# A graph network's sort and degree count: a search moved from one stage to the next

## The chip, the core and the metric
The kernel runs on one core of a Trainium2 chip. The metric is the device time of one execution in microseconds (us). The engines are named as in the profile: PE is TensorE, DVE is VectorE, ACT is ScalarE, POOL is GpSimd, SP is SyncE.

## The reference
`x` holds 12500 nodes of 16 numbers, `src` and `dst` 400000 edges between them, sorted by `dst`. The first layer runs a small MLP on each edge's two ends, makes a Householder reflection of each result, and adds messages to both ends; the second is a graph convolution applied twice. Both scale by degrees:
```
deg   = zeros(n).at[src].add(1).at[dst].add(1)          # layer 1: both ends
coef  = 1/sqrt(max(deg, 1e-5))[src] * 1/sqrt(...)[dst]
deg   = segment_sum(1, col) + 1 (self loop)             # layer 2: dst alone
norm  = rsqrt(deg)[row] * rsqrt(deg)[col]
```
Each layer is added to its input and normalized over the 16 numbers.

## The kernel before
The kernel handles gathers and scatters through a sorted order of the edges. Nodes are counted as 98 columns of 128 (`NB` = 98), two columns make a block of 256 nodes (`NW` = 49 blocks), and each of the 128 partitions holds 3125 edges (`EP`). The stages ahead of the graph layers are these.

- **Count.** The number of edges that leave each node is counted with one-hot matrices: DVE makes them for 25 edges of each partition at a time (`one_hots`, lines 1246 to 1254), ACT makes a part of them as sign steps (L694), and PE multiplies them (`count_group`, L987 and L990). There are 125 such groups (`GROUPS`) in two buffers; a DVE group waits on `hot_free` for the group two before it.
- **Search.** As `dst` is sorted, the number of edges that enter a node follows from the position of its first edge. POOL and DVE find it for all 98 x 128 nodes. PE first counts in which partition each falls (`ps_firsts`). Then there are four searches (`PROBES`), for the two halves of the 98 columns (`HALF` = 49) in 56 samples of the partition, and again for both in the 56 edges after the sample. For each, POOL issues 49 indirect DMAs (gathers, L601) into `found`, each with one index for each of the 128 partitions, and DVE compares and sums (`probe`, L1265 to L1276). DVE's loop over the groups is cut into five parts (`PAIRS`), with a search behind each of the first four, so that the gathers run beside the loop.
- **Borders.** From the first edges of every second column `cut_rows` (L1285 to L1316) finds how the edges of each block fall into rows of 5248 (`WID`); POOL gathers the keys of the edges into `keys` (41 gathers).
- **Degrees.** After the last group DVE adds the counts and makes both inverse roots, with ACT's square root in between (`rsqrt`, L1344 to L1354).
- **Sort.** Each row's 5248 keys are sorted by a merging network of 91 steps. In a step DVE takes the minimum and the maximum of two halves (L1386, L1387, two float32 inputs each) and ACT copies what doesn't move (L718, L719). The last 13 steps have no copies by ACT. `sort_stepped` counts the steps.
- **Lists.** POOL writes 99 indirect DMAs (L619) that mark where runs begin, and DVE waits for the lists (L1556).
- **Row expansion** (1420 to 2380 us): for each of 128 rows SP loads and stores about 2 MB, PE multiplies, ACT copies and DVE chooses (`choose`, L1617). SP's store of a row waits on `row_chosen`.

The graph layers follow, to the end. All order between engines is written out by hand with semaphores; each engine runs its instructions in order.

Of the kernel before, what the change touches and what calls it, by code (L numbers as in the profile page):

```python
# [11 lines left out]
def gnn_kernel(nc, x, src, dst, mlp_w1, mlp_b1, mlp_w2, mlp_b2, gcn_w1, gcn_b1, gcn_w2, gcn_b2, out):  # L12
# [9 lines left out]
    P = 128  # L22
    N, D = x.shape
# [52 lines left out]
    with ctx:  # L76
# [43 lines left out]
        dis = sb("dis", [P, NB])  # L120
        dinv = sb("dinv", [P, NB])
# [17 lines left out]
        place = sb("place", [P, WID], of=po)  # L139
        pa = ExitStack()  # L140
# [5 lines left out]
        follow = sb("follow", [P, P], of=pa)  # L146
        wrap = sb("wrap", [P, P], of=pa)
# [8 lines left out]
        found = sb("found", [P, HALF, BLOCK], of=pa)  # L156
        zeros = sb("zeros", [P, 2 * NB], of=pa)
        node_id = sb("node_id", [P, NB], of=pa)
        cum = sb("cum", [P, NB], of=pa)
        cnt = sb("cnt", [P, 2, NB], of=pa)  # L160
        start = sb("start", [P, NB + 1], of=pa)
        probe_i = sb("probe_i", [P, NB], I32, of=pa)
# [73 lines left out]
        iota_w = sb("iota_w", [P, LW], of=pb)  # L236
        pb.close()
# [82 lines left out]
        ps_edge = ps[:, 4 * BANK:4 * BANK + NB + 1]  # L320
# [35 lines left out]
        probe_ready, found_got = sem("probe_ready"), sem("found_got")  # L356
        start_ready, next_ready, edge_ready = sem("start_ready"), sem("next_ready"), sem("edge_ready")
# [21 lines left out]
        row_copied_seen, row_chosen = sem("row_copied_seen"), sem("row_chosen")  # L379
# [65 lines left out]
        sorted_keys = keys[sum(n + 1 for n in range((WID - 1).bit_length())) % 2]  # L445
        spare_keys = keys[1 - sum(n + 1 for n in range((WID - 1).bit_length())) % 2]
# [5 lines left out]
        def _(sp):  # L452
# [116 lines left out]
        def _(pool):  # L569
# [97 lines left out]
        def _(act):  # L667
# [38 lines left out]
            root(1)  # L706
            root(2)

# [15 lines left out]

            act.wait_ge(cuts_ready, 1)
# [203 lines left out]
            root(3)  # L929
# [41 lines left out]
            root(4)  # L971

        @block.tensor
        def _(pe):
# [4 lines left out]
            mm(ps_firsts, ones[:, :], hi_before[:, :], start=False, stop=True).then_inc(firsts_counted, 1)  # L979
# [12 lines left out]

            with pe.Fori(0, PAIRS[PROBES]) as i:
                for e in range(2):
                    count_group(i * 2 + e, e)
            pe.wait_ge(consts_ready, 1)
            pe.wait_ge(start_ready, 1)
            mm(ps_edge, first[:, :], start[:, :], start=True, stop=True).then_inc(edge_ready, 1)
            mm(ps_next, follow[:, :], start[:, 0:NB], start=True, stop=False)
            mm(ps_next, wrap[:, :], start[:, 1:NB + 1], start=False, stop=True).then_inc(next_ready, 1)  # L1000
            with pe.Fori(PAIRS[PROBES], GROUPS // 2) as i:
                for e in range(2):
                    count_group(i * 2 + e, e)
# [8 lines left out]
            mm(ps_rowat, ones[:, :], row_diag[:, :], start=True, stop=True).then_inc(rowat_ready, 1)  # L1012
            pe.wait_ge(runs_ready, 1)
# [191 lines left out]
        def _(dve):  # L1205
# [30 lines left out]
            v.tensor_scalar(hi_before[:, :], iota_f[:, 0:NB], first_lohi[:, 1:2], None, ALU.is_gt).then_inc(firsts_ready, 1)  # L1236
# [21 lines left out]
            dve.wait_ge(firsts_counted, 1)  # L1258
            step(v.tensor_scalar(part[:, :], ps_firsts, -1.0, 0.0, ALU.add, ALU.max))
            v.tensor_copy(probe_i[:, :], part[:, :]).then_inc(probe_ready, 1)  # L1260

            def probe(s):
                cols = slice(s % 2 * HALF, (s % 2 + 1) * HALF)
                dve.wait_ge(found_got, 16 * HALF * (s + 1))
# [17 lines left out]
            def cut_rows():  # L1282
                dve.wait_ge(keys_stored, 16)
                dve.wait_ge(edge_ready, 1)
                step(v.tensor_copy(edge[:, :], ps_edge[:, 0:NB + 1:2]))  # L1285
# [35 lines left out]
            for s in range(PROBES + 1):  # L1321
                with dve.Fori(PAIRS[s], PAIRS[s + 1]) as i:
                    for e in range(2):
                        dve.wait_ge(hot_free, i * 2 + (e - 1))
                        one_hots(e, i * (2 * T) + e * T)
# [591 lines left out]
```

## Time and profile before
| | |
|---|---|
| time, median of 3 runs | 7817.33 us (7814.12 to 7823.55) |
| span of the profiled execution | 8142.6 us |
| DVE busy | 7026.3 us, 86% |
| ACT, PE, POOL busy | 65%, 65%, 41% |
| count stage (41 to 676 us) | 635 us, DVE busy in 384.3 |
| sort (700 to 1160 us) | 460 us, DVE busy in 456.5 |

The profiled execution is one of its own, taken by the hardware profiler. Its span is 325 us longer than the median of the runs without it. Rows of the timeline give the start in us from the span's start, the duration, engine, line, operation and operands, and in brackets how long the engine had been idle and what released it. "issue" stands for idle time in which the engine waited for nothing that the profile shows, "remote" for a release whose sender the profile doesn't place on any engine.

### The profile page before, as it was taken

Reading aid. Unit: us, or ns where it says so; the run is one execution under the profiler, and the core shown is the slowest. Engines: PE = TensorE matmul, PEld = TensorE weight load, DVE = VectorE, ACT = ScalarE, POOL = GpSimd, SP = SyncE. Lnnn points to the kernel's source line nnn. Section 1 sums busy time; section 2 is a strip of 40 time slices with the busy share of each in tenths; the row PEclk is TensorE's granted clock in tenths of the full one; section 3 lists DMA queues with packets and bytes.
Section 4 is the critical chain, followed back from the end, with each engine's and each line's share of the span. In section 5 each row is a group of like instructions: output and inputs, shape, how many; then the busy total and the mean of one; then the engine's idle time right before and its main releaser. Section 6 shows DMA issues by size and latency. Waiting matters only on the chain.

```text
span 8142.6 us, 284433 instructions
## 1 busy us (share of the span) xinstructions
PE 5258.0 (65%) x105060; PEld 4635.4 (57%) x105060; DVE 7026.3 (86%) x9716; ACT 5313.1 (65%) x12774; POOL 3318.7 (41%) x2217
## 2 busy tenths in 40 slices
PE   3431000677759899999999987566466666566665
PEld 2321000566647777777777776555455566555665
DVE  6559993555559999999999999999899999999999
ACT  4534130222228888888888887888666788567886
POOL 3340006666643333333333332555200788101886
PEclk8655555888878777778777777555566555566555
DMA  3000000888863333333333332333499433697333
GB/s 45 12 20 5 0 13 13 307 292 299 294 225 99 105 105 103 104 103 104 104 105 105 105 104 84 94 85 85 112 295 296 123 94 94 199 295 237 94 94 78
DMA packets 510651, 1043.86 MB, mean 128 GB/s; under 512 B 125636, under 2 KB 316420, under 8 KB 497508
## 3 DMA queue, kind: packets, MB, share of 16 engines
q1 hardware_dynamic: 376804, 761.05, 27.3%
q0 software_dynamic: 113856, 281.66, 13.7%
q10 hardware_dynamic: 19904, 0.13, 0.2%
q8 instruction: 38, 0.62, 0.0%
q14 instruction: 49, 0.40, 0.0%
HBM read 756.40 MB, written 286.18 MB: 128 GB/s over the span
## 4 chain that ended last, share of the span: by engine, by line
DVE 32%; issue 25%; PE 21%; ACT 7%; DVEq 6%; another core or an unknown queue 3%; ACTq 2%; POOL 2%; DMA 2%; POOLq 0%; SPq 0%
PE ps L1159 11%; PE ps L1054 6%; DVE wide_hotb L1871 3%; PE ps L1193 3%; DVE keys L1387 3%; DVEq L1812 3%; ACT apartb L901 3%; DVEq L1674 2%; DVE whole L1763 2%; DVE mirr L1767 2%; DVE acc L1679 2%; DVE low L1770 2%; DVE prod L1731 2%; DVE keys L1386 2%
## 5 line engine op out<-in xcount | busy, mean ns | idle before, releaser
L601 POOL DMA_INDIRECT xs_buf<-xd_rows,src_idx x488 | 871.2, 1785 | 1809.0 <-DVE mirr L1767 1668.3
L601 POOL DMA_INDIRECT got<-val_rows,dst_idx x586 | 1045.4, 1784 | 1259.6 <-DMA val_rows<-val_out 1075.3
L1871 DVE TENSOR_SCALAR wide_hotb<-sw_inb,slot_id 128x2048 bf16<-128x2048 bf16 x976 | 922.1, 1015 | 53.0 <-PE ps L1193 52.9
L1133 PEld LDWEIGHTS ps<-w2c,hid 128*128 128x128 f32 x7808 | 942.8, 197 | 13.4
L1084 PEld LDWEIGHTS ps<-wide_tab,wide_hot 128*128 128x128 bf16 x23424 | 634.1, 102 | 521.7 <-DVE wide_hot L1664 493.7
L1133 PE MATMUL ps<-w2c,hid 128*128 128x32 f32 x7808 | 919.8, 278 | 0.0
L1670 DVE TENSOR_TENSOR lane_hotb<-rel_all,iota_b 128x3584 bf16<-128x3584 bf16 x441 | 892.8, 2025 | 11.5 <-ACT rel_all L914 7.0
L1670 DVE TENSOR_TENSOR wide_hotb<-rel_all,iota_b 128x3584 bf16<-128x3584 bf16 x438 | 886.8, 2025 | 0.2 <-ACT rel_all L914 0.2
L1159 PE MATMUL ps<-got,lane_hotb 128*128 128x48 bf16 x14112 | 642.2, 215 | 369.3 <-DVE acc L1679 187.4
L1193 PE MATMUL ps<-wide_tabb,wide_hotb 128*128 128x48 bf16 x15616 | 626.3, 205 | 369.2 <-DVE wide_hotb L1871 253.4
L1054 PE MATMUL ps<-row_tab,dst_hot 128*128 128x64 bf16 x15744 | 669.9, 204 | 273.2 <-issue 238.3
L1159 PE MATMUL ps<-got,wide_hotb 128*128 128x48 bf16 x14016 | 635.2, 214 | 321.5 <-DVE acc L1679 187.3
L1159 PEld LDWEIGHTS ps<-got,lane_hotb 128*128 128x128 bf16 x14112 | 585.6, 117 | 425.9 <-DVE acc L1679 224.4
L901 ACT ACTIVATE apartb<-iota_b,rel_negb 128x256 bf16<-128x256 bf16 x1758 | 797.6, 500 | 40.1 <-ACT rel_negb L895 0.3
L1193 PEld LDWEIGHTS ps<-wide_tabb,wide_hotb 128*128 128x128 bf16 x15616 | 580.7, 111 | 414.9 <-ACT val_out L952 341.3
L1084 PE MATMUL ps<-wide_tab,wide_hot 128*128 128x32 bf16 x23424 | 659.8, 185 | 226.0 <-DVE wide_hot L1664 222.6
L1159 PEld LDWEIGHTS ps<-got,wide_hotb 128*128 128x128 bf16 x14016 | 582.4, 117 | 374.2 <-issue 186.5
L1054 PEld LDWEIGHTS ps<-row_tab,dst_hot 128*128 128x128 bf16 x15744 | 586.8, 105 | 356.7 <-issue 333.6
L601 POOL DMA_INDIRECT src_key<-chunk_keys,src_idx x488 | 609.7, 1249 | 338.6 <-ACT xd_out L758 197.1
L758 ACT ACTIVATE xd_out<-ps 128x512 f32<-128x512 f32 (+1 forms) x384 | 199.8, 534 | 618.2 <-remote 402.9
L1617 DVE COPY_PREDICATED xd_out<-row_upper,ps 128x512 f32<-128x512 uint8 (+1 forms) x384 | 217.4, 636 | 415.2 <-ACT xd_out L758 403.4
L601 POOL DMA_INDIRECT got<-msg_rows,dst_idx x293 | 408.2, 1393 | 353.6 <-ACT rel_all L914 269.5
(392 smaller groups left out, 11976.3 us busy)
## 6 DMA issues: line engine op xcount, KB each, us to landing
dw_in<-dst_wide SPq DMA_DIRECT2D x96, 1312.0 KB
xd_rows<-xd_out SPq DMA_DIRECT2D x128, 984.0 KB
sw_in<-src_wide SPq DMA_DIRECT2D x244, 512.0 KB, 4.3
sw_inb<-src_wide SPq DMA_DIRECT2D x244, 512.0 KB, 5.1
val_rows<-val_out SPq DMA_DIRECT2D x488, 192.0 KB, 4.1
sw_inb<-src_byte SPq DMA_DIRECT2D x244, 256.0 KB
msg_rows<-msg_out SPq DMA_DIRECT2D x244, 200.0 KB, 2.4
dw_in<-dst_byte SPq DMA_DIRECT2D x32, 656.0 KB
```

The source lines that it names most:

```text
L601: return pool.indirect_dma_start(out=into, out_offset=None, in_=table, in_offset=bass.IndirectOffsetOnAxis(index, 0))
L901: last = act.activation(apart2[:, t, :], iota_b[:, :], ACT.Abs, bias=rel_neg2[:, t:t + 1])
L1054: last = mm(ps_unit[(3 * k + n) % 4][:, t - c, :, :], dst_hot[k % 2][:, t * P:(t + 1) * P], tab[:, part, :, :], start=part == 0, stop=part ...
L1084: last = mm(ps_x[:, h, t, :], wide_hot[s][:, half, e:e + P], wide_tab[s][:, h, at:at + 2 * D], start=half == part == 0, stop=half == 1 and ...
L1133: last = mm(ps_v[:, h * CH + t, :], hid[:, t % 4, at:at + P], w2c[:, :], start=False, stop=h == 1 and t == CH - 1)
L1159: last = mm(ps_sum[q][:, half * 3 * D:(half + 1) * 3 * D], lane_hot2[q][:, t, half * P:(half + 1) * P], got[q][:, at:at + 3 * D], start=t ...
L1193: last = mm(ps_val[s * 2 + h][:, t, :], wide_hot2[s][:, half, e:e + P], wide_tab2[s][:, h, half * 3 * D:(half + 1) * 3 * D], start=half == ...
L1387: return v.tensor_tensor(to_hi, lo, hi, ALU.max)
L1617: last = v.copy_predicated(xd_out[k % 4][:, c:d, 0:2 * D], row_upper[k % 4][:, c:d].unsqueeze(2).to_broadcast([P, d - c, 2 * D]), ps_unit[ ...
L1670: return v.tensor_tensor(to.rearrange("p t (j k) -> p t j k", k=2), rel.unsqueeze(2).to_broadcast(shape), iota_b[:, :].rearrange("p (j k) ...
L1812: at = dve.value_load(wide_at[0:1, 2, bass.ds(i * 4 + q, 1)], min_val=0, max_val=NW * 6 * D)
L1871: last = v.tensor_scalar(wide_hot2[q % 2][:, half, :], sw_in2[q][:, :], slot_id[:, half:half + 1], None, ALU.is_equal)
```

## The change
The block borders get a search of their own, and the search for every node moves into the sort.

- `cut_node`, `cut_below` and others search only the 50 block borders, one per partition. That takes one PE matmul with one column, two gathers (into `cut_found`) and some fifteen small DVE operations, all before the count's loop; `cut_rows` stands before the loop too.
- The count's loop is one piece. POOL's 41 key gathers are issued beside it, one for every 2.5 groups, by `hot_free`.
- The four searches of 49 gathers stand in the sort: POOL issues three gathers per sort step (waits on `sort_stepped`), DVE runs `probe(s)` behind steps 20, 40, 60 and 80 (`WAVE` = 20).
- The degrees are made at step 82 (`degrees`), the square root is one ACT instruction after the sort's copies, and the reciprocal part (`degree_factors`) follows the sort, on both kinds of degree at once.
- `row_chosen` is gone: SP waits on `unit_chosen` itself.

```diff
-        PAIRS = [1 + s * (GROUPS // 2 - 1) // (PROBES + 1) for s in range(PROBES + 2)]
+        WAVE = 20
+        STEPS = sum(n + 1 for n in range((WID - 1).bit_length()))
+        assert PROBES * WAVE + 2 < STEPS and ceil_div(HALF, 3) + 1 < WAVE
...
-                sp.wait_ge(row_chosen, i * 4 + (k + 1))
+                sp.wait_ge(unit_chosen, i * 12 + (3 * k + 3))
...
             pool.wait_ge(blocks_stored, 32)
+            for k, of in enumerate((dst_samples, dst_blocks)):
+                pool.wait_ge(firsts_ready, k + 2)
+                gather(cut_found[k][:, :], of, cut_probe[:, 0:1]).then_inc(found_got, 16)
+
+
+            pool.wait_ge(seg_ready, 1)
+            pool.wait_ge(keys_stored, 16)
+            for c in range(COLS):
+                pool.wait_ge(hot_free, 2 + 5 * c // 2)
+                gather(keys[0][:, c * P:(c + 1) * P], key_rows, seg_idx[:, c:c + 1]).then_inc(seg_got, 16)
+
+
             for s in range(PROBES):
                 pool.wait_ge(probe_ready, s + 1)
                 for h in range(HALF):
                     at = s % 2 * HALF + h
+                    if h % 3 == 0:
+                        pool.wait_ge(sort_stepped, 1 + s * WAVE + h // 3)
                     gather(found[:, h, :], dst_samples if s < 2 else dst_blocks, probe_i[:, at:at + 1]).then_inc(found_got, 16)
-
-
-            pool.wait_ge(seg_ready, 1)
-            pool.wait_ge(keys_stored, 16)
-            for c in range(COLS):
-                gather(keys[0][:, c * P:(c + 1) * P], key_rows, seg_idx[:, c:c + 1]).then_inc(seg_got, 16)
...
+            act.wait_ge(sqrt_in, 1)
+            act.activation(deg_root[:, :, :], deg[:, :, :], ACT.Sqrt).then_inc(sqrt_out, 1)
...
+            mm(ps_cut, cut_below[:, :], ones[:, 0:1], start=True, stop=True).then_inc(firsts_counted, 1)
+            pe.wait_ge(cut_edged, 1)
+            mm(ps_edge, ones[:, :], cut_diag[:, :], start=True, stop=True).then_inc(edge_ready, 1)
...
+            def cut_found_below(k):
+                dve.wait_ge(found_got, 16 * (k + 1))
+                step(v.tensor_scalar(cut_found[k][:, :], cut_found[k][:, :], cut_node[:, :], None, ALU.is_lt))
+                step(v.tensor_reduce(cut_hits[:, :], cut_found[k][:, :], AX.X, ALU.add))
...
+            dve.wait_ge(firsts_counted, 1)
+            step(v.tensor_scalar(cut_part[:, :], ps_cut, -1.0, 0.0, ALU.add, ALU.max))
+            v.tensor_copy(cut_probe[:, :], cut_part[:, :]).then_inc(firsts_ready, 1)
...
+            cut_found_below(0)
+            step(v.tensor_scalar(cut_blk[:, :], cut_hits[:, :], -1.0, 0.0, ALU.add, ALU.max))
+            step(v.tensor_scalar(cut_row[:, :], cut_part[:, :], float(BLOCKS), cut_blk[:, :], ALU.mult, ALU.add))
+            v.tensor_copy(cut_probe[:, :], cut_row[:, :]).then_inc(firsts_ready, 1)
...
-            for s in range(PROBES + 1):
-                with dve.Fori(PAIRS[s], PAIRS[s + 1]) as i:
-                    for e in range(2):
-                        dve.wait_ge(hot_free, i * 2 + (e - 1))
-                        one_hots(e, i * (2 * T) + e * T)
-                if s < PROBES:
-                    probe(s)
-                if s == PROBES - 1:
-                    cut_rows()
+            cut_found_below(1)
+            step(v.tensor_scalar(cut_row[:, :], cut_part[:, :], float(EP), cut_hits[:, :], ALU.mult, ALU.add))
+            step(v.tensor_scalar(cut_row[:, :], cut_blk[:, :], float(BLOCK), cut_row[:, :], ALU.mult, ALU.add))
+            v.tensor_scalar(cut_diag[:, :], ident[:, 0:NW + 1], cut_row[:, :], None, ALU.mult).then_inc(cut_edged, 1)
+            cut_rows()
+            with dve.Fori(1, GROUPS // 2) as i:
+                for e in range(2):
+                    dve.wait_ge(hot_free, i * 2 + (e - 1))
+                    one_hots(e, i * (2 * T) + e * T)
...
+            def degrees():
+                dve.wait_ge(next_ready, 1)
+                step(v.tensor_tensor(cnt[:, 1, :], ps_next, start[:, 0:NB], ALU.subtract))
+                step(v.tensor_tensor(deg[:, 0, :], cnt[:, 0, :], cnt[:, 1, :], ALU.add))
+                v.tensor_scalar(deg[:, 1, :], cnt[:, 1, :], 1.0, None, ALU.add)
+                step(v.tensor_scalar(deg[:, 0, :], deg[:, 0, :], DEG_MIN, None, ALU.max))
+                dve.sem_inc(sqrt_in, 1)
+
+            def degree_factors():
+                dve.wait_ge(sqrt_out, 1)
+                step(v.reciprocal(degs[:, :, :], deg_root[:, :, :]))
+                step(v.tensor_tensor(cnt[:, :, :], degs[:, :, :], degs[:, :, :], ALU.mult))
+                step(v.tensor_tensor(cnt[:, :, :], cnt[:, :, :], deg[:, :, :], ALU.mult))
+                step(v.tensor_scalar(cnt[:, :, :], cnt[:, :, :], -0.5, 1.5, ALU.mult, ALU.add))
+                step(v.tensor_tensor(degs[:, :, :], degs[:, :, :], cnt[:, :, :], ALU.mult))
...
+                    if stepped % WAVE == 0 and stepped // WAVE <= PROBES:
+                        probe(stepped // WAVE - 1)
+                    if stepped == PROBES * WAVE + 2:
+                        degrees()
```

## Rows read from the trace of the kernel before

**Rows 1.** The page: its head line and the busy time of each engine.
```profile
span 8142.6 us, 284433 instructions
...
PE 5258.0 (65%) x105060; PEld 4635.4 (57%) x105060; DVE 7026.3 (86%) x9716; ACT 5313.1 (65%) x12774; POOL 3318.7 (41%) x2217
```

**Rows 2.** Busy time by stage: count, sort, row expansion (busy us, instructions, TensorE clock, DMA share).
```profile
41.00:676.00 635.00, 252.55 (x3137) 212.41 (x3137) 384.34 (x514) 345.23 (x938) 238.88 (x237) 0.68 0.10 16
...
700.00:1160.00 460.00, 0.00 (x0) 0.00 (x0) 456.49 (x267) 73.20 (x141) 0.00 (x0) 0.50 0.01 6
...
1420.00:2380.00 960.00, 676.18 (x15760) 590.04 (x15759) 496.53 (x534) 270.19 (x640) 609.70 (x488) 0.85 0.81 293
```

**Rows 3.** The waits of 40 to 680 us (total, times, longest).
```profile
DVE step_at L1248 <- remote: 211.9, 15, 37.8
...
DVE step_at L1248 <- PE ps L990: 17.3, 7, 4.7
...
DVE step_at L1248 <- issue: 15.3, 2, 14.8
```

**Rows 4.** Timeline of TensorE and VectorE in the first search (start, duration).
```profile
56.12 0.24 PE L987 MATMUL ps<-hot_hi,hot_lo 128*128 128x98 bf16 x1 [0.24 <-issue]
...
57.53 0.24 PE L987 MATMUL ps<-hot_hi,hot_lo 128*128 128x98 bf16 x1 [1.17 <-issue]
...
80.09 0.18 DVE L1248 TENSOR_SCALAR step_at<-src_lohi 128x7 f32 x1 [25.59 <-remote]
```

**Rows 5.** Timeline of VectorE in the count without gathers.
```profile
114.45 0.16 DVE L1248 TENSOR_SCALAR step_at<-src_lohi 128x7 f32 x1
...
117.14 0.16 DVE L1248 TENSOR_SCALAR step_at<-src_lohi 128x7 f32 x1
```

**Rows 6.** Timeline of the start: a store's issue, and VectorE's third group.
```profile
22.55 0.50 SPq L460 DMA_DIRECT2D dst_blocks<-dst_f  x1
...
51.63 0.17 DVE L1248 TENSOR_SCALAR step_at<-src_lohi 128x7 f32 x1 [4.73 <-PE ps L990]
```

**Rows 7.** Timeline of VectorE: the fourth search and the border arithmetic.
```profile
530.17 3.01 DVE L1265 TENSOR_TENSOR found<-found,node_id 128x2744 f32<-128x2744 f32 x1
...
538.14 0.21 DVE L1285 COPY edge<-ps 128x50 f32<-128x50 f32 x1 [0.97 <-PE ps L998]
...
554.03 0.28 DVE L1316 TENSOR_SCALAR row_diag<-ident,row_dst 128x128 f32<-128x128 f32 x1
```

**Rows 8.** Timeline of GpSimd's gathers: one beside an idle VectorE, one beside a busy one.
```profile
59.36 0.94 POOL L601 DMA_INDIRECT found<-dst_samples,probe_i  x1 [0.30 <-issue]
...
187.39 1.35 DVE L1252 TENSOR_TENSOR hot_lo<-src_lohi,iota_b 128x2304 bf16<-128x2304 bf16 x1
...
188.52 1.04 POOL L601 DMA_INDIRECT found<-dst_samples,probe_i  x1 [0.30 <-issue]
```

**Rows 9.** DMA issues of 0 to 700 us (KB each, median us from issue to landing).
```profile
dst_blocks<-dst_f SPq DMA_DIRECT2D x1, 1568.0 KB, 7.7
...
src_list<-list_keep SPq DMA_DIRECT2D x1, 256.0 KB, 2.0
```

**Rows 10.** Timeline of VectorE between count and sort: its first and last operation there.
```profile
675.63 0.26 DVE L1350 TENSOR_TENSOR st<-cnt 128x98 f32<-128x98 f32 x1
...
681.31 0.91 DVE L1371 MEMSET list_keep<- 128x1024 f32 x1 [0.28 <-DVE dinv L1348]
```

**Rows 11.** The waits of 1160 to 1420 us.
```profile
DVE list_keep L1556 <- DMA next_row<-dst_list: 117.5, 1, 117.5
```

**Rows 12.** Timeline of VectorE in the sort: the second operation of step 20.
```profile
792.67 2.72 DVE L1387 TENSOR_TENSOR keys<-keys 128x2460 f32<-128x2460 f32 x1
```

**Rows 13.** Timeline of VectorE and GpSimd after the sort.
```profile
1277.28 3.43 DVE L1368 TENSOR_TENSOR place<-keys,parts 128x3136 f32<-128x3136 f32 x1
...
1277.67 4.98 POOL L619 DMA_INDIRECT src_list<-val_src,put_src  x1 [0.31 <-issue]
...
1280.74 1.79 DVE L1362 CAST parts<-place 128x3136 bf16<-128x3136 f32 x1
```

More of the change, by code:

```diff
@@ L139, in gnn_kernel @@
         place = sb("place", [P, WID], of=po)
+        follow = sb("follow", [P, P], of=po)
+        wrap = sb("wrap", [P, P], of=po)
+        node_id = sb("node_id", [P, NB], of=po)
+        cum = sb("cum", [P, NB], of=po)
+        cnt = sb("cnt", [P, 2, NB], of=po)
+        start = sb("start", [P, NB + 1], of=po)
+        probe_i = sb("probe_i", [P, NB], I32, of=po)
+        deg = sb("deg", [P, 2, NB], of=po)
+        deg_root = sb("deg_root", [P, 2, NB], of=po)
         pa = ExitStack()
@@ L155, in gnn_kernel @@
         hi_before = sb("hi_before", [P, NB], of=pa)
-        found = sb("found", [P, HALF, BLOCK], of=pa)
         zeros = sb("zeros", [P, 2 * NB], of=pa)
[L158 to L162, printed above, removed]
+        cut_below = sb("cut_below", [P, P], of=pa)
+        cut_node = sb("cut_node", [P, 1], of=pa)
+        cut_part = sb("cut_part", [P, 1], of=pa)
+        cut_blk = sb("cut_blk", [P, 1], of=pa)
+        cut_hits = sb("cut_hits", [P, 1], of=pa)
+        cut_row = sb("cut_row", [P, 1], of=pa)
+        cut_probe = sb("cut_probe", [P, 1], I32, of=pa)
+        cut_found = [sb(f"cut_found{k}", [P, BLOCK], of=pa) for k in range(2)]
+        cut_diag = sb("cut_diag", [P, NW + 1], of=pa)
         src_lohi = [sb(f"src_lohi{h}", [P, EP, 2], BF16, of=pa) for h in range(2)]
@@ L236, in gnn_kernel @@
         iota_w = sb("iota_w", [P, LW], of=pb)
+        found = sb("found", [P, HALF, BLOCK], of=pb)
         pb.close()
@@ L928, in _ @@
             keys_turn(G2 // 4, 0)
-            root(3)
+            root(2)
             for l in range(2):
@@ L970, in _ @@
                 act.activation(node_h[:, 0:NB, :], agg[:, :, :], ACT.Tanh).then_inc(tanh_out, 1)
-            root(4)
+            root(3)
         @block.tensor
@@ L991, in count_group @@
                 last.then_inc(hot_free, 1)
-            with pe.Fori(0, PAIRS[PROBES]) as i:
-                for e in range(2):
[L995 to L1001, printed above, removed]
+            with pe.Fori(0, GROUPS // 2) as i:
                 for e in range(2):
@@ L1012, in _ @@
             mm(ps_rowat, ones[:, :], row_diag[:, :], start=True, stop=True).then_inc(rowat_ready, 1)
+            pe.wait_ge(start_ready, 1)
+            mm(ps_next, follow[:, :], start[:, 0:NB], start=True, stop=False)
+            mm(ps_next, wrap[:, :], start[:, 1:NB + 1], start=False, stop=True).then_inc(next_ready, 1)
             pe.wait_ge(runs_ready, 1)
@@ L1257, in _ @@
             part, blk, hits, row = st
-            dve.wait_ge(firsts_counted, 1)
-            step(v.tensor_scalar(part[:, :], ps_firsts, -1.0, 0.0, ALU.add, ALU.max))
-            v.tensor_copy(probe_i[:, :], part[:, :]).then_inc(probe_ready, 1)
             def probe(s):
                 cols = slice(s % 2 * HALF, (s % 2 + 1) * HALF)
-                dve.wait_ge(found_got, 16 * HALF * (s + 1))
+                dve.wait_ge(found_got, 16 * (2 + HALF * (s + 1)))
                 step(v.tensor_tensor(found[:, :, :], found[:, :, :], node_id[:, cols].unsqueeze(2).to_broadcast([P, HALF, BLOCK]), ALU.is_lt))
@@ L1284, in cut_rows @@
                 dve.wait_ge(edge_ready, 1)
-                step(v.tensor_copy(edge[:, :], ps_edge[:, 0:NB + 1:2]))
+                step(v.tensor_copy(edge[:, :], ps_edge))
                 step(v.tensor_copy(edge_i[:, :], edge[:, :]))
@@ L1320, in _ @@
                 one_hots(e, e * T)
-            for s in range(PROBES + 1):
-                with dve.Fori(PAIRS[s], PAIRS[s + 1]) as i:
-                    for e in range(2):
-                        dve.wait_ge(hot_free, i * 2 + (e - 1))
-                        one_hots(e, i * (2 * T) + e * T)
-                if s < PROBES:
-                    probe(s)
-                if s == PROBES - 1:
-                    cut_rows()
+            cut_found_below(1)
[7 more added lines that the diff above has]
+                    one_hots(e, i * (2 * T) + e * T)
             dve.wait_ge(hot_free, GROUPS - 2)
             one_hots(0, (GROUPS - 1) * T)
-            dve.wait_ge(next_ready, 1)
-            step(v.tensor_tensor(cnt[:, 1, :], ps_next, start[:, 0:NB], ALU.subtract))
+            step(v.tensor_scalar(part[:, :], ps_firsts, -1.0, 0.0, ALU.add, ALU.max))
+            v.tensor_copy(probe_i[:, :], part[:, :]).then_inc(probe_ready, 1)
             dve.wait_ge(counted, 1)
@@ L1855, in _ @@
             step(v.memset(node_h[:, :, :], 0.0))
-            step(layernorm(3, node_h[:, 0:NB, :], agg[:, :, :]))
+            step(layernorm(2, node_h[:, 0:NB, :], agg[:, :, :]))
             v.tensor_copy(node_x[:, 0:NB, :], node_h[:, 0:NB, :]).then_inc(nt_in, 1)
```

38 lines of the change are left out of this document (15 added, 23 removed).

## The prediction

> **What bounds the kernel now.** I read the page first: VectorE (DVE) is busy 86% of the span [rows 1]. Then the table by stage, for where it is not. Two stages hold most of its idle time: the degree count from 41 to 676 us, 384 of 635 us busy, and the row expansion (1420 to 2380 us), 497 of 960 us busy with the DMA engines at 0.81 [rows 2]. The sort between them leaves DVE 3.5 us idle in 460. So one microsecond of DVE costs one microsecond in the sort and in an undisturbed count, and nothing in the row expansion.
>
> In the waits of the count DVE waits 212 us for "remote", which is no engine [rows 3]. The timeline shows what that is. While GpSimd (POOL) issues gathers back to back, TensorE starts one instruction per 0.7 us (or a multiple of it), waiting for nothing, and DVE gets its next release 25 us later though TensorE's previous group is over [rows 4]. Without gathers a group of 25 edges takes 2.69 us and DVE never waits [rows 5]. The stalls are 212 + 17 + 15 = about 244 us.
>
> Are these stalls in a timed run too? The profiled span is 8142.6 us, the median of the runs 7817.3: 325 us of the profiled execution are not in a timed one. They have to come out of DVE's idle time, 8142.6 - 7026.3 = 1116 us, since the durations of busy instructions don't shrink. The row expansion can give at most 0.19 x 960 = 182 us before the DMA engines are full [rows 2]. So at least some 140 us must be missing elsewhere, and the count's 244 us with no cause on any engine are the one block that large. ScalarE (ACT) runs its steps beside the stutter at full speed; only TensorE, which has by far the most instructions to record, ticks. I take it that the recording makes the stalls, and that in a timed run the count goes at DVE's pace.
>
> **The change part by part**, as a timed run would have it.
>
> *The count, before.* DVE starts the loop at 51.6, having waited 4.7 us for the first group [rows 6]. Then 122 groups x 2.685 = 327.6 us, four searches x 7.1 (the fourth begins at 530.17 and its last operation is over at 537.2, [rows 7]) = 28.4, four loop restarts x 0.3 = 1.2, the edge wait 1.0, the border arithmetic 538.14 to 554.3 = 16.2 [rows 7], the last group 2.7. One wait is hidden in the profile by the stalls: beside a DVE that never pauses a gather comes every 1.34 us [rows 8], so 49 take 65.7, with 0.4 to start and 1.5 to land (estimate from the 2.0 us of a small store, [rows 9]) 67.6 us, against 12 iterations x 5.37 + 0.7 = 65.1 us of cover: 2.5 x 3 = 7 us. It ends near 435.8.
>
> *The count, after.* Nine small operations before the loop and four at the first search's end, 13 x 0.22 = 2.9 us. The first border gather waits for the block store (issued at 22.55, [rows 6], 7.7 us to land, [rows 9]), so its result is there at about 33.7, when the second cast that covers it ends at 33.0: 0.7. The key store is issued 2.8 us later, lands near 52, and the border arithmetic waits 1.5 us for it. It ends at about 68.3, and its length also covers the 4.7 us wait. Then 327.6 + 2.7: 398.6. The 41 key gathers come one per 2.5 groups, 6.7 us for 1.34 us of work, over by group 102 of 125; hidden. Difference -37 us.
>
> *Between count and sort.* The two square-root chains, 675.63 to 681.31, go: -5.7 [rows 10]. The new first index (0.5 us) stands inside DVE's wait for TensorE's last group, which is longer. The four operations of `degrees` inside the sort cost +1.1; the reciprocal part (five on 196 columns, about 3 us) moves into DVE's wait of 117.5 us for the lists [rows 11]: 0. If that cover were gone it would be 3 us. ACT's square root comes after its last copy and has nine sort steps of 460/91 = 5 us to finish in.
>
> *The searches in the sort.* DVE's part is as long as before: +28.4. The 196 gathers are the risk. What does a gather do beside DVE? In the count each one that starts inside a two-input DVE operation ends 0.82 us after that operation's end: 188.52 + 1.04 = 189.56 against 187.39 + 1.35 = 188.74 [rows 8]. It is held until the boundary and gets one slot there; the next starts 0.30 later, inside the next operation. Alone a gather takes 0.94 and the next comes after 1.25 us [rows 8]. So POOL makes one gather per DVE operation, however long that is. In the count these last 1.34 us, in the sort up to 2.9: step 20 is two operations of 2.72 us, two boundaries [rows 12]. A wave has the 19 steps from the end of step 20s+1 to the end of 20s+20. The pacing lets 3 gathers go per step; I expect 2. That is 38 of 49, and the other 11 go at 1.25 each with DVE waiting: 13.8 + 1.5 = 15.3 us for waves 1 and 2. Wave 3 ends in steps of 4 to 6 short operations and needs about 12, wave 4 about 7: together +50.
>
> That float32 two-input operations hold a gather is bounded by rows, too: one started 0.39 us into such an operation and took 4.98, until 0.12 after the cast behind it [rows 13]. Bounds: 0 if min/max on two float32 tiles does not hold it, 50 by the boundary rule, and about 37 us per wave, 130 in all, if the boundary inside a step (min to max, overlapped by 0.08) grants nothing and only the step's end does. I take 50: 188.52 shows a grant at an overlapped boundary.
>
> The Trainium skill (SBUF — State Buffer, Who interferes with whom) says that a VectorE instruction with two SBUF inputs contends with a GpSimd instruction that reads SBUF, and that the second to issue fully blocks. By that rule every min and max of the sort holds a gather; the trace agrees for two bf16 inputs [rows 8]; no gather here starts well inside an operation with two float32 ones. By the rule the sum is the one below, without it 50 us less.
>
> *The row expansion.* One DVE wait less per row; DVE is 48% idle there and the DMA engines bound it. A store goes out at most 0.1 us earlier, and each buffer's turn is four rows: -1, bounds 0 and -3.
>
> Sum: -37 - 5.7 + 1.1 + 28.4 + 50 - 1 = +36, so 7853 us. (The profiled span should fall all the same: 671.6 to about 399 in the count, +79.5 in the sort, near 7940.)
>
> **The rivals.**
> - *The stalls are real in timed runs.* Then the count loses its 244 us, the hidden waits (7) were not there, and the 4.7 is already in the 244: -273 - 5.7 + 79.5 - 1 = -200, 7617 us. For it: DVE's release, not only TensorE's records, is late. Against it: the 325 us would have to come from elsewhere. The Trainium skill (NOTIFIC — the notification-queue block, Constraints, capacities, measured rates) says that emitting a record costs the engine nothing; by that the stalls are real, while its section Interfaces lets a full FIFO stall an engine, by which they are not. A part of them (a third) would give about 7750. This is the case on the other side.
> - *Gathers are not held by the sort's operations.* 3 per step, 48 by step 17, done before step 20: no wait, 7803 us. For it: no row shows a gather begun inside an operation with two float32 inputs; against it: [rows 8, 13], where bf16 with bf16 and float32 with bf16 hold one.
> - *Only the step's end grants.* 49 gathers in 19 slots: +130 in place of 50, 7935 us.
> - *The new wait for the key store is long.* The store would have to land after 52 by more than the whole +36 to matter; 7.7 us for one as large makes 5 us the most.
>
> **How the numbers follow.** 0.2% is 15.6 us, about what a measurement of this kernel can tell from no change. Chances: forecast 0.60 (own range 7838 to 7872: landing time, searches and small operations +-10, grants +-10); not held 0.15; step's end only 0.07; stalls real in full 0.12, in part 0.06. Slower: 0.57 of the first and 0.07: 0.64. Same: 0.03 of the first and 0.09 of the second: 0.12. Faster: 0.18 and 0.06: 0.24. The range 7760 to 7910 takes the first two cases and part of the third's and the partial stall's edges: some 0.78.
>
> **What would show it.** In the profile after: the count over near 400 us with "remote" almost gone; gathers in the sort that take 2 to 2.9 us in place of 0.94, two per step; DVE idle before L1265's comparison at steps 20, 40, 60, 80, about 15, 15, 12, 7 us, with POOL at 1.25 us per gather inside these waits; no search work in the count. Wrong, if DVE does not wait there (7803), or if the timed gain follows the profiled span down (7617).

## The result, and the profile after

The changed kernel takes 7845.22 us (median of 5 runs, 7838.58 to 7855.56) against 7817.33 (7807.32 to 7823.55): ratio 1.0039, 95% interval 1.0028 to 1.0050. It is 0.4% slower, +28 us; +36 was forecast. A second measurement of the pair gave 7839.44 and 7816.83, ratio 1.0031 (1.0019 to 1.0044).

But that is half of the result. On two of the four chips that the further runs met, the kernel before takes 8127 and 8157 us in its timed runs too, and on the second of these, where the pair was timed, the change makes it 2.2% faster (ratio 0.9781, 0.9749 to 0.9812). The text below calls these chips the second kind and the two others, with 7815 and 7817 us, the first kind. The profile from which the prediction was made has a span of 8142.6 us, which fits only the second kind, while the 7817 us beside it are those of the first. On which chip it was taken is not on record, so this is an inference.

The page of the changed kernel, by its time on a chip of the first kind. The span is 1.7 us below this execution's own time of 7842.12.

```profile
span 7840.4 us, 284410 instructions
## 1 busy us (share of the span) xinstructions
PE 5091.5 (65%) x105062; PEld 4533.1 (58%) x105062; DVE 7001.7 (89%) x9725; ACT 5283.6 (67%) x12773; POOL 3517.7 (45%) x2219
```

Its stages, to be held against [rows 2]: the count, the sort with the searches, and the row expansion (columns as there).

```profile
41.00:410.00 369.00, 228.29 (x3135) 194.87 (x3135) 362.12 (x496) 342.08 (x937) 49.31 (x41) 0.79 0.04 12
410.00:950.00 540.00, 1.17 (x4) 0.93 (x4) 477.17 (x277) 68.38 (x134) 353.85 (x196) 0.50 0.10 12
1230.00:1960.00 730.00, 526.76 (x15643) 499.59 (x15641) 465.17 (x532) 238.69 (x636) 549.42 (x406) 0.94 0.96 382
```

In the count VectorE is busy 362 of 369 us. The sort, which had it busy almost throughout, now leaves 63 us idle. The waits there, VectorE's own for what the searches gathered (total, times, longest):

```profile
DVE found L1296 <- DMA found<-dst_samples,probe_i: 36.6, 2, 19.3
DVE found L1296 <- DMA found<-dst_blocks,probe_i: 22.1, 2, 13.5
```

That is 58.7 us in four waits. The timeline shows how a wave of gathers runs: first beside two sort steps, then in the wait before the first search's comparison.

```profile
456.74 2.89 DVE L1425 TENSOR_TENSOR keys<-keys 128x2624 f32<-128x2624 f32 x1
457.85 2.61 POOL L616 DMA_INDIRECT found<-dst_samples,probe_i  x1 [0.30 <-issue]
459.55 2.88 DVE L1426 TENSOR_TENSOR keys<-keys 128x2624 f32<-128x2624 f32 x1
460.76 2.50 POOL L616 DMA_INDIRECT found<-dst_samples,probe_i  x1 [0.30 <-issue]
...
523.02 0.94 POOL L616 DMA_INDIRECT found<-dst_samples,probe_i  x1 [0.30 <-issue]
524.27 0.95 POOL L616 DMA_INDIRECT found<-dst_samples,probe_i  x1 [0.30 <-issue]
...
538.03 0.95 POOL L616 DMA_INDIRECT found<-dst_samples,probe_i  x1 [0.31 <-issue]
541.22 3.02 DVE L1296 TENSOR_TENSOR found<-found,node_id 128x2744 f32<-128x2744 f32 x1 [19.32 <-DMA found<-dst_samples,probe_i]
```

The gather begun at 457.85 ends at 460.46, 0.83 us after min is over at 459.63, and the next ends 0.83 after max: two per step, each 2.5 to 2.6 us long. From 523.02, beside an idle VectorE, one comes every 1.25 us, 13 of them, and the result of the last is there at 541.22, 2.2 us after that gather's end at 538.98.

### The profile page after: what moved, and what is told of

Same layout as the page of the kernel before. It is cut to its first block, busy times and chain, and to the rows that moved or that the text cites. A ratio compares the mean times of both kernels' runs of the same rounds, so it can differ in the third digit from the quotient of the medians.

```text
span 7840.4 us, 284410 instructions
## 1 busy us (share of the span) xinstructions
PE 5091.5 (65%) x105062; PEld 4533.1 (58%) x105062; DVE 7001.7 (89%) x9725; ACT 5283.6 (67%) x12773; POOL 3517.7 (45%) x2219
## 4 chain that ended last, share of the span: by engine, by line
DVE 26%; issue 23%; POOL 13%; ACT 11%; PE 11%; DMA 9%; DVEq 5%; ACTq 2%; SPq 0%; POOLq 0%
DMA xd_rows<-xd_out 6%; POOL got L616 6%; PE ps L1179 6%; POOL found L616 4%; DVE wide_hotb L1913 3%; PE ps L1213 3%; ACT apartb L923 3%; DVEq L1716 3%; ACT step_lo L717 2%; DVE whole L1805 2%; DVE mirr L1809 2%; DVE low L1812 2%; DVE prod L1773 2%; DVE acc L1721 2%; POOL src_key L616 2%
## 5 line engine op out<-in xcount | busy, mean ns | idle before, releaser
L616 POOL DMA_INDIRECT src_key<-chunk_keys,src_idx x488 | 628.7, 1288 | 220.0 <-issue 166.5
L1074 PE MATMUL ps<-row_tab,dst_hot 128*128 128x64 bf16 x15744 | 522.6, 197 | 200.4 <-DVE xd_out L1661 129.6
L1074 PEld LDWEIGHTS ps<-row_tab,dst_hot 128*128 128x128 bf16 x15744 | 498.7, 101 | 224.6 <-DVE xd_out L1661 139.6
L882 ACT ACTIVATE hid<-ps,b1c 128x1024 f32<-128x1024 f32 x488 | 516.9, 1118 | 4.1 <-PE ps L1138 4.1
L964 ACT ACTIVATE wide_tabb<-parts 128x96 bf16 x976 | 276.0, 283 | 361.3 <-issue 278.5
```

The source lines that it names most:

```text
L616: return pool.indirect_dma_start(out=into, out_offset=None, in_=table, in_offset=bass.IndirectOffsetOnAxis(index, 0))
L882: act.activation(hid[:, :, at], ps[:, 0:4 * BANK].rearrange("p (b c) -> p b c", b=4)[:, :, at], ACT.Relu, bias=b1c[:, :]).then_inc(hid_rea ...
L964: last = act.activation(wide_tab2[q % 2][:, h, :], parts[:, bass.ds(at, 6 * D)], ACT.Copy)
L1074: last = mm(ps_unit[(3 * k + n) % 4][:, t - c, :, :], dst_hot[k % 2][:, t * P:(t + 1) * P], tab[:, part, :, :], start=part == 0, stop=part ...
```

## The experiments

**The kernel before, profiled again.** No edit.

> The kernel before, unchanged, for a second profile. If the recording makes the stalls of the count, this profile shows them again: the last sort prelude near 680 us, DVE waiting some 210 us for 'remote', a row expansion of some 960 us and a span near 8140. If they were an accident of one profiled execution, the count is over near 436 us, 'remote' holds under 10 us, the row expansion takes some 730 us, and the span is near the timed 7817. The time outside the profile should be 7817 either way.

Time 8110.16 us, span 8108.4, and in 23 timed runs on that chip 8127.47 (8095.62 to 8162.90). The next lines are the head of the page, the largest wait of the count, and three tiles with their durations (min/median/max in ns) and their first and last start. VectorE writes `hot_hi` last in each group of the count, clears `xd_out` when the row expansion begins, and makes the first `wide_hot` when it is over.

```profile
span 8108.4 us, 284433 instructions
DVE step_at L1248 <- remote: 137.6, 16, 32.2
L1252 DVE TENSOR_TENSOR hot_hi<-src_lohi,iota_b x125: 1422/1430/1441, 42.8 to 632.3; 128x2450 bf16<-128x2450 bf16 x125
L1603 DVE MEMSET xd_out<- x4: 1698/1698/1698, 1393.6 to 1399.8; 128x1968 f32 x4
L1664 DVE TENSOR_SCALAR wide_hot<-sw_in,slot_id x488: 734/749/789, 2375.3 to 5004.1; 128x2048 bf16<-128x2048 bf16 x163
```

Neither outcome that I had set down: the stalls are back, and the timed runs on that chip are as long as the profiled execution, which lies inside their range. So the 325 us are not what a profiled execution takes more than a timed one on the same chip.

**And once more, on a chip of the first kind.**

> The kernel before, unchanged, for one more profile. On a chip where it takes 7817, by my theory of the count: the sort's first steps begin near 463 us in place of 681 (count over near 436, no DVE wait for 'remote', only some 7 us for the gathers of the searches), and the row expansion lasts some 720 us at 380 GB/s or more. If it takes 7817 with the stalls of the count in it, the time was lost elsewhere in the first profile.

Time 7817.35 us, span 7815.6. The same views:

```profile
span 7815.6 us, 284189 instructions
DVE found L1265 <- DMA found<-dst_blocks,probe_i: 27.3, 2, 24.9
DVE found L1265 <- DMA found<-dst_samples,probe_i: 3.3, 1, 3.3
L1252 DVE TENSOR_TENSOR hot_hi<-src_lohi,iota_b x125: 1417/1425/1430, 42.8 to 459.5; 128x2450 bf16<-128x2450 bf16 x125
L1603 DVE MEMSET xd_out<- x4: 1698/1698/1698, 1220.6 to 1226.8; 128x1968 f32 x4
L1664 DVE TENSOR_SCALAR wide_hot<-sw_in,slot_id x488: 734/745/782, 2086.4 to 4711.0; 128x2048 bf16<-128x2048 bf16 x163
```

No wait for "remote". The last group of the count starts at 459.5 in place of 632.3 (173 us), the row expansion, from the first xd_out to the first wide_hot, lasts 866 us in place of 982 (116 us). The other stages differ by 4 us. This execution was profiled like the other, so the profiler alone does not make the stalls. But VectorE waits 30.6 us for the searches' gathers where I had worked out 7. The timeline of the third search shows why:

```profile
227.19 1.35 DVE L1252 TENSOR_TENSOR hot_lo<-src_lohi,iota_b 128x2304 bf16<-128x2304 bf16 x1
228.33 2.38 POOL L601 DMA_INDIRECT found<-dst_blocks,probe_i  x1 [0.30 <-issue]
228.45 1.43 DVE L1252 TENSOR_TENSOR hot_hi<-src_lohi,iota_b 128x2450 bf16<-128x2450 bf16 x1
229.87 1.34 DVE L1252 TENSOR_TENSOR hot_lo<-src_lohi,iota_b 128x2304 bf16<-128x2304 bf16 x1
```

A gather that begins 0.2 us before a boundary gets nothing from it and is held until the next: it ends at 230.71, 0.83 after hot_hi. Then the following one begins 0.2 us before the next boundary again. Sixteen gathers in a row, from 223.17 to 265.91, took some 2.67 us each in place of 1.34: 21 us, most of the 24.9 us wait. Before them GpSimd paused for 3.2 us with no cause that the profile shows.

**The changed kernel again**, on the same chip.

> The changed kernel, unchanged. On a chip where the kernel before takes 7817: 7845 again. On a chip where the kernel before takes 8127: near 7971 (no_search's 7884 there and the 87 us that the searches cost in the sort), so 1.9% faster than the kernel before; its gathers beside the count are 41 and come one per 6.7 us, and beside the sort TensorE has nothing to do. If instead the searches' gathers cost more there, it takes over 8000.

7839.44 us, ratio 1.0031 (1.0019 to 1.0044). Its span is 7837.4 us. With the profile above this is the pair that the ledger below is made of:

```profile
DVE found L1296 <- DMA found<-dst_samples,probe_i: 35.3, 2, 18.0
DVE found L1296 <- DMA found<-dst_blocks,probe_i: 21.8, 2, 13.5
L1286 DVE TENSOR_TENSOR hot_hi<-src_lohi,iota_b x125: 1421/1427/1433, 44.2 to 402.0; 128x2450 bf16<-128x2450 bf16 x125
L1647 DVE MEMSET xd_out<- x4: 1698/1698/1698, 1243.8 to 1250.0; 128x1968 f32 x4
L1706 DVE TENSOR_SCALAR wide_hot<-sw_in,slot_id x488: 735/745/885, 2110.1 to 4731.9; 128x2048 bf16<-128x2048 bf16 x163
```

**The changed kernel on a chip of the second kind.**

> The changed kernel, unchanged, for its time on a chip of the other kind, if this call gets one. Where the kernel before takes 8127: near 7971 (no_search's 7884 there and the 87 us that the searches cost in the sort), 1.9% under it; if gathers cost more beside the sort there, over 8000. Where the kernel before takes 7817: 7842 again, which tells nothing new.

7980.03 us against 8157.26, ratio 0.9781 (0.9749 to 0.9812). Its span is 7984.9 us; its count is as short as on the other chips, its row expansion is not:

```profile
L1286 DVE TENSOR_TENSOR hot_hi<-src_lohi,iota_b x125: 1421/1429/1435, 44.3 to 402.2; 128x2450 bf16<-128x2450 bf16 x125
L1647 DVE MEMSET xd_out<- x4: 1698/1698/1698, 1246.3 to 1252.4; 128x1968 f32 x4
L1706 DVE TENSOR_SCALAR wide_hot<-sw_in,slot_id x488: 743/748/796, 2251.1 to 4877.7; 128x2048 bf16<-128x2048 bf16 x163
```

The last group at 402.2 where the kernel before, on the other chip of this kind, has it at 632.3: 230 us won, of which the sort's +83 (844.1 from there to the first xd_out, against 761.3) takes its part.

**The searches left out of the sort.** (Chip of the second kind.)

```diff
-            for s in range(PROBES):
-                pool.wait_ge(probe_ready, s + 1)
-                ... (49 gathers)
-                        probe(stepped // WAVE - 1)
+                        if stepped // WAVE == PROBES:
+                            step(v.memset(start[:, 0:NB], 0.0))
+                            dve.sem_inc(start_ready, 1)
```

> The changed kernel with the four searches left out of the sort: their 196 gathers and VectorE's work on what they bring are gone, the first indices are set to zero, so the in-degrees are not the reference's and nothing else changes. By my theory the searches cost the sort their VectorE work (28.4) and the four waits that the profile shows (58.7): 87 us less than the changed kernel's 7845, so near 7758. If the waits were an effect of the recording alone, only the work goes: near 7817. If gathers also slowed VectorE's sort operations, more than 87 goes.

7884.46 us against 8127.47 there, ratio 0.9708 (0.9683 to 0.9734). The absolute time that I had named was for the other kind of chip. The price is read from the stage: from the last group of the count to the first xd_out.

```profile
L1279 DVE TENSOR_TENSOR hot_hi<-src_lohi,iota_b x125: 1420/1429/1434, 44.5 to 402.2; 128x2450 bf16<-128x2450 bf16 x125
L1642 DVE MEMSET xd_out<- x4: 1698/1698/1698, 1161.3 to 1167.4; 128x1968 f32 x4
```

759.1 us, against 844.1 with the searches (on the other chip of this kind): 85.0, where 87 were expected. The waits are real time. The gathers cost the sort's own operations nothing that shows: a minimum over 2624 columns takes 2.892 us in the changed kernel and 2.893 here.

**The row edit alone**, put into the kernel before.

```diff
-                sp.wait_ge(row_chosen, i * 4 + (k + 1))
+                sp.wait_ge(unit_chosen, i * 12 + (3 * k + 3))
-                dve.wait_ge(unit_chosen, i * 12 + (3 * k + 3))
-                dve.sem_inc(row_chosen, 1)
```

> The kernel before with one edit alone: the store of an expanded row waits for the three units of its row by their own semaphore, and VectorE's wait and increment after each row are gone. By my theory 0 to -3 us (VectorE is idle for half of that stretch and the transfers bound it): the same within 0.2%. The rival: the wait held VectorE at each of some 120 rows, and its going explains the shorter row expansion in the profile of the changed kernel; then the time falls by tens of us and this profile's row expansion takes some 730 us.

8128.39 us against 8127.47, ratio 1.0005 (0.9989 to 1.0022): no difference. The row expansion takes 992 us here, against 982 in the profile of the kernel before on this chip. The shorter row expansion in the first profile of the changed kernel is not the edit's: the kernel before has it too on a chip of the first kind (866 us).

**All four searches back beside the count**, with the early border search kept. (Chip of the second kind.)

```diff
+            PAIRS = [1, 24, 37, 50, GROUPS // 2]
+            for s in range(PROBES):
+                with dve.Fori(PAIRS[s], PAIRS[s + 1]) as i:
+                    ...
+                if s < PROBES - 1:
+                    probe(s)
```

> The changed kernel with the node search moved back beside the degree count: three searches between count groups with some 13 iterations each to cover their 49 gathers, the fourth's work at the head of the sort, the key gathers right after the border gathers and before the node searches; early border search, the shorter square-root chain and the row edit stay. By my sum it keeps border search early (no arithmetic under the wait for the first group, -4.7 and the rest of it +2.9 +0.8), the square roots (-4.6) and the hidden waits of the old count (-7): about 14 us under the kernel before, near 7803. If the stalls of the first profile were in timed runs, gathers beside the count would cost here as before, and the time would be near the kernel before (7817) or above.

8117.51 us against 8127.47, ratio 0.9998 (0.9976 to 1.0020), with 115 us of waits for "remote" in the count. This is the second case of the expectation: on such a chip gathers back to back beside the count stall it again (the last group starts at 590.1), and the time is that of the kernel before. What it gives on a chip of the first kind was not run.

**More steps per search.**

```diff
-        WAVE = 20
+        WAVE = 22
```

> The changed kernel with 22 sort steps per search in place of 20. By my theory (about two gathers per step, one slot at each boundary of VectorE's operations, and VectorE waits at 1.25 us per gather for those left) two more steps take four gathers more per wave before VectorE waits: about 5 us less in each of the first three waves, up to 18 us in all: near 7829. If the waits are the latency of a wave and not the slots left over, nothing changes: 7845.

7820.91 us, ratio to the kernel before 1.0009 (1.0000 to 1.0018), and 22 us under the run of the next paragraph, which shares its chip and has the waits of the changed kernel. Waits in its sort:

```profile
DVE found L1296 <- DMA found<-dst_samples,probe_i: 27.8, 2, 15.5
DVE found L1296 <- DMA found<-dst_blocks,probe_i: 9.7, 2, 8.8
```

37.5 us in place of 57.3: a step more is two gathers fewer to wait for.

**No pacing.**

```diff
-                    if h % 3 == 0:
+                    if h == 0:
```

> The changed kernel with the pacing of the gathers in the sort left out: only the first gather of each wave waits for its step. By my theory the boundaries of VectorE's operations let two gathers go per step, while the pacing allows three, so it never holds: 7845, within 5 us, and waits of the same lengths before steps 20, 40, 60 and 80. The rival, that the pacing is what holds the gathers back, gives shorter waits, down to -59 us (7786). A third: gathers queued deeper slow other transfers of the sort, and the time rises.

7842.68 us, ratio to before 1.0034 (1.0022 to 1.0046), waits of 35.3 and 22.0 us. The pacing holds nothing back; VectorE's operations do.

**Which operations hold a gather.** Five times 12 gathers, the first four beside VectorE operations of 2.8 to 2.9 us.

```diff
+            for n in range(5):
+                dve.sem_inc(tanh_in, 1)
+                for m in range(14 if n < 4 else 0):
+                    ... n == 0: v.tensor_tensor(to, half, rest_of, ALU.min)
+                    ... n == 1: v.tensor_reduce(to[:, 0:41], half..., AX.X, ALU.min)
+                    ... n == 2: v.tensor_tensor(to, a..., ps_wide_in, ALU.min)
+                    ... n == 3: v.tensor_copy(b[:, :], a[:, :])
+                dve.wait_ge(found_got, 16 * (2 + 12 * (n + 1)))
```

> The changed kernel with a measurement put in ahead of the sort: five times 12 gathers of 128 rows, the first four beside 14 VectorE operations each, the fifth beside an idle VectorE. A: min of two float32 SBUF tiles (2624 columns, some 2.8 us); B: a reduction of one float32 tile (2624 columns); C: min of a float32 tile and a PSUM tile (2548 columns); D: a float32 copy of 5248 columns. My theory: in A one gather per operation, each ending about 0.8 us after its operation's end, so that gathers come every 2.8 us; in B and C one every 1.25 us as beside the idle engine (E), since there is one SBUF input; D is held as A if the copy runs in a fast mode, else as B. The rival, that a gather is held by any VectorE operation, gives one gather per operation in B and C too. The added work makes the time longer by some 150 us; only the durations inside count.

From the timeline of blocks A to D:

```profile
428.74 11.54 DVE L1440 TENSOR_TENSOR keys<-keys 128x2624 f32<-128x2624 f32 x4
429.95 2.50 POOL L616 DMA_INDIRECT found<-dst_samples,probe_i  x1 [0.30 <-issue]
432.75 2.62 POOL L616 DMA_INDIRECT found<-dst_samples,probe_i  x1 [0.30 <-issue]
...
466.19 11.39 DVE L1442 TENSOR_REDUCE keys<-keys 128x41 f32<-128x2624 f32 x4 [0.18 <-DVE keys L1440]
467.61 0.94 POOL L616 DMA_INDIRECT found<-dst_samples,probe_i  x1 [0.31 <-issue]
...
506.34 8.37 DVE L1444 TENSOR_TENSOR keys<-keys,ps 128x2548 f32<-128x2548 f32 x3 [0.18 <-DVE keys L1442]
507.75 0.94 POOL L616 DMA_INDIRECT found<-dst_samples,probe_i  x1 [0.30 <-issue]
...
548.34 11.68 DVE L1447 COPY keys<-keys 128x5248 f32<-128x5248 f32 x4
551.66 5.55 POOL L616 DMA_INDIRECT found<-dst_samples,probe_i  x1 [0.30 <-issue]
```

A: one gather per operation. B and C, with one input from SBUF: 0.94 us and one per 1.25, as beside an idle engine. So the rival, that any VectorE operation holds a gather, fell. D is worse than I expected: one gather per two copies, 5.55 us, though a copy reads one tile only.

**Two searches in the count, two in the sort.** The version that the waits point to.

```diff
+            PAIRS = [1, 24, 46, GROUPS // 2]
...
+                    if s < 2:
+                        pool.wait_ge(hot_free, 2 + 4 * issued // 5)
...
+                    if stepped in (36, 72):
+                        probe(1 + stepped // 36)
```

> The changed kernel with the first two node searches back beside the degree count, their gathers and the key gathers paced at one per 0.8 of a count group (2.15 us), and the last two in the sort, 36 steps each in place of 20. By my theory the four waits of the sort (58.7 us) go, since 36 steps have room for some 70 gathers at two per step, and nothing new waits in the count: on a chip where the kernel before takes 7817 it takes 7786, less than both kernels. On a chip where the kernel before takes 8127, its back-to-back gathers beside the count make TensorE start an instruction only every 0.7 us; if paced gathers do not do that, it takes near 7910 there (no_search's 7884 and the searches' 28), and if they do, more by up to 190.

The edit paces the gathers of the first two searches and the key gathers. Those of the last two searches wait for their indices alone, so the third search's gathers begin beside the end of the count.

7783.49 us (7775.91 to 7786.48), ratio to the kernel before 0.9954 (0.9940 to 0.9967), and 56 us under the changed kernel on the same chip. In its sort no wait for the searches' gathers is left; in the count VectorE waits 1.1 us for TensorE.

**The same on a chip of the second kind.**

> The kernel with two searches in the count and two in the sort, unchanged. Where the kernel before takes 8127: near 7910 if gathers paced at 2.15 us leave TensorE alone, up to 8100 if they bring back the starts 0.7 us apart. Where the kernel before takes 7817: 7783 again.

7971.84 us, ratio to the kernel before 0.9779 (0.9746 to 0.9812), the changed kernel's 0.9781 again. The waits of its count:

```profile
DVE step_at L1284 <- remote: 25.0, 7, 4.5
DVE step_at L1284 <- PE ps L1017: 18.6, 12, 4.5
```

The last group starts at 461.5 in place of 414.2, 47 us later. Do the paced gathers bring back these stalls? The table by stretch (columns as in [rows 2]) says that they do not:

```profile
67.00:170.00 103.00, 65.04 (x925) 56.46 (x925) 102.67 (x115) 101.86 (x281) 57.13 (x48) 0.79 0.18 13
232.00:390.00 158.00, 97.93 (x1400) 87.68 (x1400) 156.57 (x174) 151.57 (x414) 88.44 (x70) 0.74 0.14 22
392.00:465.00 73.00, 27.88 (x322) 25.23 (x320) 33.19 (x35) 32.69 (x91) 56.86 (x50) 0.52 0.10 20
```

In the first two stretches, with gathers one per 2.1 to 2.3 us, VectorE is busy but for 0.3 and 1.4 us. In the third it is idle for 40 us of 73: there the unpaced gathers of the third search run back to back. Another 7 us are lost from 204 to 214, where the second search's gathers make up for a late start and also go back to back. So the first case of the expectation holds for the pacing, and its 7910 was missed mainly because the third search is not paced. A version that holds that search until the sort was not run; by these rows it would save some 40 us on such a chip (an estimate). As it stands the kernel gives back in the count what it wins in the sort there, and so beats the kernel before on both kinds of chips and the changed one on the first.

## Why the prediction was right, and where it was not

The direction, the mechanism and the time held: 7853 forecast, 7845 measured. The sum looks better than its terms, and that is luck: two of them were too small with opposite signs, by 20.5 and 6.9 us. The ledger, from the pair of profiles on one chip (differences of the last group's start, of the first xd_out, the first wide_hot and the end):

| stage | forecast | measured |
|---|---|---|
| count | -37 | 402.0 - 459.5 = -57.5 |
| between count and rows, the sort in it | -5.7 + 1.1 + 28.4 + 50 = +73.8 | 841.8 - 761.1 = +80.7 |
| row expansion | -1 | 866.3 - 865.8 = +0.5 |
| the rest | 0 | -1.9 |
| sum | +36 | +21.8 (medians: +22.6 there, +27.9 in the first measurement) |

*The count before.* "2.5 x 3 = 7 us" of hidden waits was the mis-sized term: 30.6 us. The count's last group ended at 460.9, 25.1 later than forecast, and this term is 23.6 of it. "One gather per boundary" left out that a boundary can be missed, and that the missing repeats itself.

*The count after* ended 5 us later than the 398.6 that I gave. The loop began at 67.0 (forecast 68.3), but its 122 groups took 334.4 us in place of 327.6: most at 2.69, some fifteen of 2.94 to 3.10.

*The waits in the sort*, forecast 15, 15, 12 and 7: 19.3, 17.3, 13.5 and 8.6. The rule of one gather per boundary, and so two per step, is what the timeline and block A show. The first wave had 13 gathers left, not 11: two of its gathers (4.68 and 4.77 us long) each lost a boundary, and why these did, begun 1.4 and 1.5 us ahead of it, is open. The last result takes 2.2 us to land, not 1.5. With 28.4 for the work, 1.1 and -5.7 the measured 57.1 of that pair make +80.9, and +80.7 was found.

*The square roots and the row edit* came out as said. *The key store* made no wait.

*The rivals.* "Not held" fell: block A and the run without searches. "Only the step's end grants" fell: two gathers per step.

The rival of stalls that are real in part has a slip in its sum: a third of the way from 7853 to 7617 is 7774, not 7750.

*The stalls.* "I take it that the recording makes the stalls" is the step that failed. Its consequence, that the timed 7817 holds none, was right, and so the forecast stood; that was luck, for its cause was wrong. The argument noticed that 325 us of the profiled execution were in no timed run and that the count's stalls had to be most of it (211 us: its last group at 670.3 against 459.5), and then took the one difference that it knew of, the profiler, for the reason. That the two numbers could come from two chips did not occur to me as a third case. A step of the same argument failed too: that the row expansion can give at most 182 us, since the DMA engines are busy in 0.81 of it. From the first to the last `choose` it takes 925 us in the profile before and 709 on a chip of the first kind, 217 less. Of that 92 us go to the wait behind it, for GpSimd's gathers into `src_key`: 96.2 us there in place of 4.1.

What the runs show is this. A profiled execution of the kernel before has no wait for "remote" on one chip, where it takes 7817.35 us against a median of 7816.83 in the timed runs. On another it has them, with 8110.16 us against timed runs of 8095.62 to 8162.90. So the recording alone does not make the stalls. Two things stay open. Every timed run in the results has a span and a granted clock of its own, so it may have been recorded as well, and a recording that costs time only on such chips is not ruled out. And each chip was met only once, one after the other: whether the chip differs, or something about it at that time, as for example the load of other cores, was not tested. The timed runs of the kernel before spread over 49 and 67 us on the second kind and over 15 and 19 us on the first.

The rival "the stalls are real in timed runs" is what happens on chips of the second kind: forecast -200 there, measured -177.

The two rules of the Trainium skill came out so. NOTIFIC — the notification-queue block, section Constraints, capacities, measured rates: that a record costs the engine nothing agrees with the profiled 7817.35 us beside the timed 7816.83, as far as those timed runs were not recorded. SBUF — State Buffer, section Who interferes with whom: two SBUF inputs contend, one does not outside the two-port modes, and a reduction on this chip never does; blocks A, B and C agree. The page also recalls a probe in which two-input operations did not stall a DMA issued by GpSimd; here gathers were stalled by them (2.5 us in place of 0.94), and the measurement decides. For float32 copies its section 🔬 SBUF: two separate sides has GpSimd locked out while the copy runs; block D agrees that copies hold a gather, and there it took the time of two.

## What to carry to other kernels

GpSimd's gathers run at full speed beside a VectorE reduction and beside a minimum whose second input is in PSUM (blocks B and C). Float32 copies, which also read one SBUF tile only, hold them longest (block D). Beside two-input operations count operations, not microseconds: at most one gather per boundary, whether the operation lasts 1.3 or 2.9 us. So many gathers belong beside many short operations, or spread thin over both stages, and every one of them has to be paced: in the last version, on a chip of the second kind, it was mostly the one unpaced search that cost the time. And when a profile and the times beside it disagree by 4%, first profile again and time on that same chip, before a cause is looked for in the profiler: the sign of a change can hang on the chip.

## What the runs showed of the hardware

- Two kinds of chips, or of conditions on a chip. The same kernel takes 7815 to 7817 us on two of the four, as in the first measurement, and 8127 and 8157 on the other two. On the second kind the row expansion moves 293 GB/s in place of 377 to 382 with the DMA engines less busy (0.81 against 0.96), and while gathers are issued back to back beside the count TensorE starts an instruction per 0.7 us or a multiple. With 41 gathers one per some 7 us it did not (last group at 402.2), nor with one per 2.1 us (VectorE busy in 102.67 of 103 us). What differs, and why gathers reach TensorE there, stays open.
- A gather begun some 0.2 us before a boundary can miss it, and the miss repeated 16 times while the operations kept their period.
- Beside back-to-back float32 copies of 2.89 us a gather takes 5.55 us and ends 0.12 us after a copy's end, while beside two-input operations it mostly takes one boundary and ends 0.82 after it.
